# Eight output buffers for routed tiles, two tail gates moved into the experts' drain, table sums moved between units, output by batch

## What is computed

```python
scores = softmax(xt @ Wg.T)                      # 2048 tokens, 16 experts
topi = top_k(masked, 4)                          # 4 experts for each token, from 2 of 4 groups
h = silu(einsum('td,eid->eti', xt, W1)) * einsum('td,eid->eti', xt, W3)   # inner width 176
expert_out = einsum('eti,edi->etd', h, W2)
y = einsum('etd,te->td', expert_out, combine)
z = silu(xt @ Ws1.T) * (xt @ Ws3.T) @ Ws2.T      # shared expert, inner width 352 = 2 units of 176
out = x + y + z
```

## Time and profile before

| | us |
|---|---|
| median of 3 runs | 426.54 |
| lowest and highest run | 420.03, 428.16 |
| profiled execution, its own time | 423.51 |
| its span in the trace | 421.4 |

### The profile page before, as it was taken

How to read it: one execution, slowest core, us unless ns; L and a number is a source line. 1 busy time by engine, 2 the same in 40 slices (tenths; PEclk the granted TensorE clock), 3 DMA queues, 4 the chain that set the end, 5 groups by cost and what they waited for, 6 DMA issues and landing times.

```text
span 421.4 us, 9784 instructions
## 1 busy us (share of the span) xinstructions
PE 342.2 (81%) x2395; PEld 232.1 (55%) x2396; DVE 256.5 (61%) x982; ACT 217.2 (52%) x553; POOL 188.4 (45%) x223
## 2 busy tenths in 40 slices
PE   1698988789898944558998899888989899896676
PEld 0475755456666732335775666565656556554355
DVE  4467687876787778557553555554554454557671
ACT  0666677656755642423664555554554554554440
POOL 1553422127647655873650245454545445446200
PEclk9996596665655675586999999999999999999699
DMA  8812123114333434434624667785555645579922
GB/s 290 293 40 81 59 71 109 61 60 143 115 115 115 140 119 126 156 120 153 217 96 68 103 152 155 142 117 124 133 122 118 138 103 133 136 239 339 291 100 101
DMA packets 82060, 57.87 MB, mean 137 GB/s; under 512 B 58858, under 2 KB 75501, under 8 KB 82032
## 3 DMA queue, kind: packets, MB, share of 16 engines
q1 hardware_dynamic: 63600, 39.60, 35.2%
q0 software_dynamic: 6912, 17.84, 12.8%
q10 hardware_dynamic: 11520, 0.09, 2.3%
HBM read 24.58 MB, written 24.53 MB: 117 GB/s over the span
## 4 chain that ended last, share of the span: by engine, by line
PE 42%; DVE 15%; issue 13%; DMA 5%; ACT 4%; POOL 3%; POOLq 1%; SPq 1%; another core or an unknown queue 1%; DVEq 1%; ACTq 0%
PE bank L735 16%; PE bank L750 12%; DMA ranked<-ctx_all 3%; PE bank L743 3%; PE bank L741 2%; DVE x_all L1361 2%; PE bank L865 2%; DVE hid L1214 2%; POOL slot_rows L1435 1%; ACT hh L547 1%; DVE hh L1219 1%; PE bank L616 1%; PE bank L742 1%; PE bank L623 1%; POOL rs L1414 1%
## 5 line engine op out<-in xcount | busy, mean ns | idle before, releaser
L1463 POOL DMA_INDIRECT ranked<-ctx_all x80 | 81.0, 1012 | 92.6 <-ACT ctx_all L589 66.1
L750 PE MATMUL bank<-w,hT 128*128 (+3 forms) x560 | 82.3, 279 | 12.3 <-ACT ctx_all L589 6.0
L735 PE MATMUL bank<-w,ctx_all 128*128 x480 | 85.1, 313 | 2.6 <-issue 2.1
L1435 POOL DMA_INDIRECT slot_rows<-rows_all,slot_k x64 | 65.5, 1023 | 27.9 <-issue 14.9
L750 PEld LDWEIGHTS bank<-w,hT 128*128 128x128 f16 (+1 forms) x560 | 51.0, 99 | 36.0 <-issue 25.1
L542 ACT ACTIVATE silu<-bank 128x176 f32<-128x176 f32 x112 | 35.4, 316 | 50.2 <-PE bank L735 23.8
L547 ACT ACTIVATE hh<-hid 128x176 f16<-128x176 f32 x112 | 39.1, 349 | 30.0 <-DVE hid L1214 17.7
L1218 DVE TENSOR_TENSOR hh<-hid,hh 128x48 f16<-128x48 f32 x112 | 23.4, 209 | 50.5 <-ACT hh L547 31.8
L735 PEld LDWEIGHTS bank<-w,ctx_all 128*128 128x128 f16 x480 | 42.2, 97 | 21.4 <-issue 4.7
L1347 DVE COPY hT<-bank 128x384 f16<-128x384 f16 x80 | 28.2, 353 | 35.3 <-PE bank L743 26.9
L589 ACT ACTIVATE ctx_all<-bank,ctx_all 128x256 f32<-128x256 f32 x80 | 37.6, 470 | 17.8 <-PE bank L750 12.3
(11 more groups left out here) (145 smaller groups left out, 568.4 us busy)
## 6 DMA issues: line engine op xcount, KB each, us to landing
wst<-w_dram SPq DMA_DIRECT2D x18, 608.0 KB
w<-ranked SPq DMA_DIRECT2D x16, 512.0 KB, 10.4
slot_rows<-pad_rows SPq DMA_DIRECT2D x17, 144.0 KB
x_all<-x_dram SPq DMA_DIRECT2D x4, 512.0 KB
out_dram<-x_all SPq DMA_DIRECT2D x4, 512.0 KB, 2.9
ctx_all<-ctx_dram SPq DMA_DIRECT2D x1, 1536.0 KB, 10.3
ctx_all<-slot_rows SPq DMA_TRANSPOSE x80
ctx_all<-slot_rows ACTq DMA_DIRECT2D x80, 1.0 KB
```

What stands on the lines that cost most here:

```text
L735: i = mm(U[j][:, 0:UP1], xt(2 * part + k), w[:, span(wcol + wpart * WH + k * UP1, UP1)], start=k == 0 and (wpart, part) == (0, 0), stop=k ...
L750: i = mm(y[:, 0:T], hT[0:rows, j, k * P:(k + 1) * P], w[0:rows, span(col, T)], start=start and n == 0, stop=stop and n == len(parts) - 1)
L1435: G.indirect_dma_start(scatter_rows, bass.IndirectOffsetOnAxis(ap=slot_k[:, b * TOPK + k:b * TOPK + k + 1], axis=0), rows32[:, b * ROW32:( ...
L1463: G.indirect_dma_start(ranked, bass.IndirectOffsetOnAxis(ap=pair(m)[1], axis=0), y_sb[:, m % YR, :], None, bounds_check=(TOPK + 1) * TOKEN ...
```

## The change

- `YR` goes from 4 to 8. The semaphores' counts follow: in the loop ACT still waits for tile s-8, in the drain for t-8 in place of t-4. `stored[k]` is now rounded up to a multiple of 8 tiles. `meta` gets a buffer of its own, since eight result buffers fill the reused area.
- ACT's gates of tail units 24 and 25 move from the tail to steps NT+1 and NT+2 of the routed tiles (steps 81 and 82).
- PE's `count` moves from after step 4 to inside step 5, after `up` of unit 5 and before the transposes of unit 3.
- PE's 16 table matmuls are spread: `tables` puts 2, 4, 3 and 3 of them after the steps n = 27, 29, 31 and 33 of the tail (the ranks 0, 1 and 2); the four of rank 3 stand at the end.
- The last four batches are stored one by one (128 KB each), each after its own add.

```diff
-        YR = 4
+        YR = 8
...
-        meta = reuse(MR * 2)
+        meta = sb("meta", [P, MR * 2])
...
-            for n in range(B // CB):
-                if CB * n < B1:
-                    sp.wait_ge(acc_done, n + 1)
-                else:
-                    sp.wait_ge(SH["y_ready"], B)
+            for n in range(B1 // CB):
+                sp.wait_ge(acc_done, n + 1)
                 sp.dma_start(ov[:, CB * n:CB * n + CB, :],
                              x_all[:, CB * n * T:CB * (n + 1) * T].rearrange("p (b t) -> p b t", t=T)).then_inc(S["out_written"], 16)
-            sp.wait_ge(S["out_written"], 16 * B // CB)
+            for b in range(B1, B):
+                sp.wait_ge(SH["y_ready"], b + 1)
+                sp.dma_start(out[b], x_all[:, span(b * T, T)]).then_inc(S["out_written"], 16)
+            sp.wait_ge(S["out_written"], 16 * (B1 // CB + B - B1))
...
-                if shared(n, 0, first, last):
+                if shared(n, 0, first, last) and not (tail and n < 2 * first + 2):
                     gate(SH, n, n % 2, n % (2 if tail else UF))
...
-                        wait(act, y_out[m], 4 * (t - m))
+                        wait(act, y_out[m], 2 * (t - m))
...
-                        act.wait_ge(y_out[v], 4 * (s - MR - v) + 16)
+                        act.wait_ge(y_out[step_v % MR], 2 * (s - MR - step_v % MR) + 16)
...
-            expert_pipeline(act, estep, 5)
+            def turn(s, step_v, r):
+
+                estep(s, step_v, r)
+                if r is None and s in (NT + 1, NT + 2):
+                    n = 2 * B1 + s - NT - 1
+                    gate(SH, n, n % 2, n % 2)
+
+            expert_pipeline(act, turn, 5)
...
+                if n == 5:
+                    count(B - Q)
                 if shared(n, T_LAG[0], first, last):
...
-                if stage == "S" and n == 4:
-                    count(B - Q)
...
-            shared_units(pe, last_units, B1, B, 2, lambda stage, n: None)
-
-            def sum_parts(b):
-
-                for k in range(TOPK):
-                    if b == B1:
-                        pe.wait_ge(*part_in(b // CB, k))
+            added = [0]
+
+            def add_tables(b, *ks):
+
+                for k in ks:
+                    if k >= added[0]:
+                        pe.wait_ge(*part_in(B1 // CB, k))
+                        added[0] = k + 1
                     i = mm(YS[b - B1][:, 0:T], ident, part(b // CB, k)[:, b % CB * T:(b % CB + 1) * T], start=False, stop=k == TOPK - 1)
-                i.then_inc(sum_mm, 1)
-
+                if TOPK - 1 in ks:
+                    i.then_inc(sum_mm, 1)
+
+            def tables(stage, n):
+
+                b = n // 2 - 1
+                if n % 2 == 1 and b >= B1:
+                    add_tables(b, 0, 1)
+                    for a in range(B1 if b == B1 + 1 else b, b + 1 if b > B1 else b):
+                        add_tables(a, 2)
+
+            shared_units(pe, last_units, B1, B, 2, tables)
             for b in range(B1, B):
-                sum_parts(b)
+                add_tables(b, 3)
```

More of the change, by code:

```diff
@@ L261, in build @@
         sum_mm = sem("sum_mm")
-        FFN = "xt_mm xt_ready up_mm silu_ready h_ready hhi_ready hlo_ready ht_mm hT_ready dn_mm y_ready".split()
+        FFN = "up_mm silu_ready h_ready hhi_ready hlo_ready ht_mm hT_ready dn_mm y_ready".split()
         SH = {n: sem(f"sh_{n}") for n in FFN}
```

## The result

| | before | after |
|---|---|---|
| median of 20 runs, us | 426.39 | 420.54 |
| lowest and highest, us | 420.03, 429.24 | 417.13, 423.77 |
| profiled execution, own time and span, us | 423.51, 421.4 | 421.31, 419.0 |
| ratio of the compared runs, 95% interval | | 0.9924 [0.9897, 0.9950] |

The ratio says minus 3.2 us (2.1 to 4.4); the medians are 5.85 apart, the means of all 20 runs 5.1.

What follows compares the result with a forecast made beforehand. It took ACT's landing waits to bound the drain, DVE the tail and PE's table sums the end. 1.75 + 2.95 + 1.1 = 5.8 us off gave 417.7 or 420.7, middle 419.2 us, range 414 to 424.

Steps and rivals of the forecast that it cites:

- drain term: Drain, 383 to 392 us: eight buffers and early gates leave DVE's adds last, minus 1.75 us; bounds 0 to 1.8.
- A second reading of the term: Drain: ACT's four scalings then wait for PE's downs alone, so ACT ends between 387.5 and 388.5, not 392.1.
- The base: Start of the sum: middle of 417.7 (from the profiled execution) and 420.7 (from the median), giving 419.2 us.
- Tables between units: Tail and end: nine table matmuls leave the end, 3.89 us, DVE loses 0.93; net minus 2.95 us.
- Output by batch: End: the last store is 128 KB instead of 512; minus 1.1 us, from 0 to 1.4.
- rival D: End: the small stores come one after another, 3 us more than overlapped, 423 us; chance 0.04.
- Count: PE's count behind up of unit 5: zero, at most +0.5 us, at best 0.4 gained.
- SP's longer wait: Before the 9th table load SP waits 3.75 us more; taken as 0, bounds 0 and +1.8 us.
- rival A: Loads late: SP's longer wait goes through, plus 1.75 us at the 13th load, 421.2 us; chance 0.13.
- Rival B: Tail at the low clock: PE's clock doesn't come back after the drain, 13 us added, 432 us; chance 0.06.
- Rival C: ACT stays late in the drain or table matmuls push DVE; 1 to 2 us gain left, 424 us; chance 0.10.

Runs made afterwards that it cites:

- again_before: The kernel before, repeated without an edit: ratio 1.0008 [0.9962, 1.0055].
- fine_waits_b: The changed kernel with SP's waits before the table loads on exact instead of rounded-up counts, run for a second trace: 421.82 us in one run.
- groups 3 and 4: Comparisons of SP's exact against rounded-up waits (group 3: exact in the change 0.9878, rounded-up in before 1.0001) and of candidates side by side (group 4).
- full_side: The whole changed kernel once more, without a further edit, on one chip with two variants: ratio to before 0.9884 [0.9843, 0.9924], median 416.97 us.
- group 4: Side by side against before on one chip: the change 0.9884, the change without its drain part 0.9884, the change with exact waits 0.9917.
- coarse_before: The kernel before, with SP waiting for the rounded-up 64, 64, 72 and 72 tiles as the change does: ratio 1.0001 [0.9965, 1.0037].
- exact waits: The changed kernel with SP's waits before the table loads for 60, 64, 68 and 72 tiles, not rounded up: ratios to before 0.9878 and 0.9917.
- full_side_b: One more trace of the whole changed kernel, without a further edit: 410.08 us in one run.

## Why the prediction was wrong, and where it was right

**The drain term is the step that failed:** "Minus 1.75". Its mechanism is right as far as it goes: eight buffers and early gates make DVE's adds the last to finish, and where nothing delays DVE the drain shrinks by 2.2. The step that fails is that DVE's adds would begin when they began before: the lower bound, "at least 0 (if the adds begin later)", had no price and no chance. In five of nine traces they do begin later, by 1.8 to 2.5; in four of them because DVE stands still with its input ready, in the fifth mostly because PE is at its lower clock. Before, the landing waits of ACT covered such a delay (in `again_before` the copy comes 1.7 late and the drain is 9.30), and those waits are what the edit removed. For the whole term the runs' ratios showed about 0 in place of 1.75, and the traces' mean says 1.0.

A second reading of the term was off without harm: ACT's scalings don't wait for PE's downs alone. In the four traces without a delay the last one waits for `meta` and ends 6.1 to 6.3 after the load of tile 79, where 4.4 to 5.4 was forecast, still before the adds end at 7.4 to 7.5.

Two readings of that stay open. The first is whether eight buffers bring pauses or only uncover them. DVE's copies and ACT's silus stop for about 2 us, with no releaser known, in most of the traces, before included. In before, in DVE's timeline of the routed loop:

```profile
286.71 0.36 DVE L1347 COPY hT<-bank 128x384 f16<-128x384 f16 x1 [2.04 <-remote]
```

The longest of DVE's in the routed loop, 3.03, is at 341.36 in `fine_waits_b`. At tile 79's copy a pause with the input ready for over 1 us shows in 5 of 10 traces with eight buffers and in 1 of 7 with four; that at least five of the six would fall to the ten by chance has a probability of 0.16. So it isn't shown that eight buffers bring pauses; that they uncover a delay is.

The second is what the pause is. It is not pure chance, for it has places: ahead of tile 58's copy DVE idles for 1.8 to 2.1 in 16 of the 17 traces, whatever the buffers, in seven of them with no releaser known. That POOL's writes hold DVE up isn't what the rows show: before's copy at 385.64 starts in the middle of one (385.14 to 386.12) without delay. SP's burst is neither needed for a pause (`again_before` has none of it) nor enough (groups 3 and 4); that it makes one likelier isn't excluded. The Trainium skill, "Runtime: NRT & Kernel Launch", section "Instruction fetch mechanics", tells of a stall after a taken branch whose target isn't in the engine's small instruction memory. No run here shows that, and I didn't try it. The packets of the instruction queues don't fall on the pauses: in after the nearest one is seen between 392.5 and 393, and the pause had ended at 389.3; in `full_side` it is seen between 389.0 and 389.5, and the pause had ended at 387.4.

**The base was the second fault.** I took the middle of a sum from the profiled execution (417.7) and one from the median (420.7). Of the 7.3 us by which 419.2 lies below the median 426.54, 5.8 were terms and 1.5 the choice of base. The run of after that was profiled took 421.31, not 417.7. Without the drain term the sum is 4.05, between the 3.2 of the result's ratio and the 4.9 of group 4's. A gain has to be forecast from the number that it is compared with.

**Tables between units: right.** Forecast -2.95; the tail went from 25.74 to 22.53 in the profiled pair, and from 25.9 (before, its repeat, `coarse_before`) to 23.0 (the three with spread sums and the old drain) in the mean, -2.9. Alone it gave 0.9918 for a forecast 0.993. `hidden` of unit 30 waits 0.61 for its silu where 0.9 was expected.

**Output by batch: right.** -0.99 for -1.1; the small stores land in 1.8 and overlap, so rival D falls (it wanted 3 more). The Trainium skill, "DMA: Bandwidth & Descriptors", section "Anatomy of one DMA", would give an estimate of 2.3 for each, but its fit is for transfers that GpSimd issues, and these are SP's; the row, 1.7 to 1.9 from issue to landing, is below that, and the row decides.

**Count: right.** The first reader stands at 190.91, 4.66 after DVE's write of the choices that the count reads (186.25), where before it was 4.53 (192.25 and 187.72), and the transposes on PE still wait for DVE (1.04).

**SP's longer wait: right at 0,** and rival A falls. SP's 9th load goes out at 383.89 in after. The DMA share stays high about a us longer (0.98 at 399 to 400, 0.31 at 400 to 400.5), but no reader waits for a table, and `coarse_before` gives 1.0001.

**Rival B** had a piece of truth: the clock did fall before the last sums, which cost 1.46 us, but in the two kernels that keep the sums in one block behind an idle PE. With the sums spread it stayed at 1.00 from 404 to 417 in after.

**Rival C** said that ACT would stay late or that the table sums would push DVE. Neither happened; that its 1 to 2 us of gain are nearer to the ratio's 3.2 than the forecast's 7.3 is luck. The loss came by a way that no rival named.

The version without the drain part (0.9894, 0.9884) is, within these intervals, as fast as the whole change (0.9924, 0.9943, 0.9884) and as exact waits (0.9878, 0.9917), and it needs neither the four further buffers nor the moved gates.

## What to carry to other kernels

When an edit removes the latest of several waits, look in more than one trace at what the second latest does: here it was late by about 2 us in five of nine executions, and the old wait had covered it. Price such delays from the rows where they already stand (a pause of 2.04 was in the trace of before, in the routed loop), and give them a chance. A matmul block that runs alone at the end is worth spreading between units with slack: that gave 2.9 of the 4 us, and TensorE's clock was never at its lower level ahead of the last sums in the eleven traces with spread sums, while it was in two of the six with the block.

## What the hardware showed that I had not expected

- DVE and ACT stand still for about 2 to 3 us, in most executions, with no releaser in the trace: 2.70 at 389.31 in after (the input was ready for 2.4 of it), 2.50 on ACT at 386.50 in `again_before`. In the changed kernel tile 79's copy has the pause in three traces of five; before tile 58's copy DVE idles for 1.8 to 2.1 in 16 of all 17 traces.
- The same 1.32 us of idle time on PE is followed by a fall of the granted clock to 0.5 in two traces and by full clock in four others.
- ACT's last scaling reads `meta`, a load of 1 KB issued by the last `load_pair`. Once the landing waits are gone it is what ACT waits for last in the four traces without a delay; in ACT's timeline of `full_side_b`, 5.7 us after its issue at 375.06:

```profile
380.80 0.47 ACT L589 ACTIVATE ctx_all<-bank,meta 128x256 f32<-128x256 f32 x1 [1.97 <-DMA meta<-slot_rows]
```
